# Cross-attention and expert layer: setup and attention loop laid out anew over five batches a step

## The reference, cut to what matters

```python
x = x + attention(layernorm(x), ctx, mask, Wq, Wk, Wv, Wo)   # x: 16 x 256 x 128, ctx: 16 x 64 x 128
x = x + experts(layernorm(x), gate_w, wi_gate, wi_up, wo)

def attention(H, T, mask, Wq, Wk, Wv, Wo):                   # 16 heads of 8
    q, k, v = shape(H @ Wq) * 8 ** -0.5, shape(T @ Wk), shape(T @ Wv)
    scores = q @ k.T + (1 - mask) * finfo.min
    return (softmax(scores) @ v) @ Wo

def experts(x, ...):                                         # 8 experts, F = 512, top 2
    probs, idx = top_k(softmax(x @ gate_w.T), 2); probs /= sum(probs)
    for k in range(2):                                       # capacity 640 tokens for each k and expert
        pos = running count of the tokens that chose the same expert
        out += where(pos < 640, probs[k] * (silu(x @ wi_gate) * (x @ wi_up)) @ wo of expert idx[k], 0)
```

## Time and profile before

| | |
|---|---|
| median of 3 runs | 415.29 us (413.87 to 417.47) |
| profiled execution, its own time | 416.42 us |
| its span, first to last instruction | 414.6 us |
| mean granted TensorE clock | 0.946 |
| busy: TensorE, DVE, GpSimd, ACT | 359.5, 259.9, 228.2, 189.4 us |

### The profile page before, as it was taken

The page is one execution under the profiler, slowest core; times in us unless marked ns, Lnnn a source line. Parts: engine busy times, 40 slices in busy tenths (PEclk is TensorE's granted clock), DMA queues, the critical chain, the costliest instruction groups (busy, mean ns, idle before and its releaser), DMA issues.

```text
span 414.6 us, 8885 instructions
## 1 busy us (share of the span) xinstructions
PE 359.5 (87%) x3012; PEld 311.1 (75%) x3012; DVE 259.9 (63%) x893; ACT 189.4 (46%) x430; POOL 228.2 (55%) x190
## 2 busy tenths in 40 slices
PE   0776889999989999648499999999999999999980
PEld 0465567667766676337399999999999999999980
DVE  4947868988898989754144545565554546555430
ACT  2435647667757677422132443443443434344320
POOL 9514421035337757877207648386565837747664
PEclk9969959999999999967799999999999999999996
DMA  8898010122212322111503444636345463544332
GB/s 257 249 326 280 6 31 14 20 48 73 39 43 67 83 74 72 60 58 54 148 4 26 91 97 38 162 33 146 48 53 140 37 161 26 121 73 37 29 28 25
DMA packets 41958, 35.05 MB, mean 85 GB/s; under 512 B 9136, under 2 KB 38320, under 8 KB 41776
## 3 DMA queue, kind: packets, MB, share of 16 engines
q1 hardware_dynamic: 27824, 24.72, 21.2%
q0 software_dynamic: 13568, 9.58, 16.9%
q10 hardware_dynamic: 528, 0.27, 0.2%
HBM read 21.64 MB, written 17.73 MB: 95 GB/s over the span
## 4 chain that ended last, share of the span: by engine, by line
PE 64%; DVE 17%; POOL 7%; issue 5%; DMA 2%; ACT 2%; POOLq 0%; DVEq 0%; ACTq 0%
PE bank L820 17%; PE bank L629 10%; PE bank L631 9%; PE bank L630 9%; POOL slots L443 6%; PE bank L706 4%; DVE mneg L925 3%; PE bank L658 2%; PE bank L672 2%; DVE rall L1044 2%; PE bank L685 2%; PE bank L811 2%; PE bank L793 1%; PE bank L686 1%; PE bank L696 1%
## 5 line engine op out<-in xcount | busy, mean ns | idle before, releaser
L477 POOL DMA_INDIRECT out<-ys,idx x80 | 124.9, 1561 | 84.4 <-DVE ys L1123 36.8
L1150 DVE TENSOR_TENSOR h<-sg,bank 128x256 f32<-128x256 f32 x160 | 66.0, 417 | 87.5 <-ACT sg L614 79.2
L614 ACT ACTIVATE sg<-bank 128x256 f32<-128x256 f32 x160 | 61.6, 385 | 108.1 <-PE bank L631 107.2
L629 PE MATMUL bank<-ex_hi,w_hi 128*128 128x256 f32 x320 | 96.1, 300 | 1.1 <-DVE ex_lo L1104 0.3
L630 PE MATMUL bank<-ex_hi,w_lo 128*128 128x256 f32 x320 | 89.7, 280 | 0.0
L631 PE MATMUL bank<-ex_lo,w_hi 128*128 128x256 f32 x320 | 89.7, 280 | 0.0
L820 PE MATMUL bank<-w_raw,h 128*128 128x128 f32 x640 | 78.0, 275 | 0.8 <-DVE h L1150 0.8
L820 PEld LDWEIGHTS bank<-w_raw,h 128*128 128x128 f32 x640 | 74.9, 192 | 0.9 <-DVE h L1150 0.9
L443 POOL DMA_INDIRECT slots<-rall,slot x64 | 64.0, 1000 | 19.6 <-issue 15.2
L629 PEld LDWEIGHTS bank<-ex_hi,w_hi 128*128 128x128 f32 x320 | 61.1, 191 | 4.2 <-issue 2.5
L630 PEld LDWEIGHTS bank<-ex_hi,w_lo 128*128 128x128 f32 x320 | 61.2, 191 | 0.0
(11 more groups left out here) (120 smaller groups left out, 540.5 us busy)
## 6 DMA issues: line engine op xcount, KB each, us to landing
slots<-in_empty SPq DMA_DIRECT2D x8, 660.0 KB, 10.1
xl<-slots SPq DMA_DIRECT2D x7, 660.0 KB, 6.8
w_raw<-in_wgu SPq DMA_DIRECT2D x8, 512.0 KB, 3.8
X<-in_x SPq DMA_DIRECT2D x4, 512.0 KB, 7.7
w_raw<-in_wdn SPq DMA_DIRECT2D x8, 256.0 KB, 4.3
out<-X SPq DMA_DIRECT2D x16, 128.0 KB
out<-ys,idx POOLq DMA_INDIRECT x80, 3.3
ks<-kc SPq DMA_DIRECT2D x72, 16.0 KB
```

What stands on the lines that cost most here:

```text
L477: nc.gpsimd.indirect_dma_start(out=out[:, :], out_offset=bass.IndirectOffsetOnAxis(ap=IDX[v][:, j:j + 1], axis=0), in_=YS[c][:, t, :], in_ ...
L614: nc.scalar.activation(SG[m % 2][:], GATE_PS[m % 2][:, 0:2 * P], ACT.Silu).then_inc(sg_ready, 1)
L629: nc.tensor.matmul(ps, hi, m_hi, start=True, stop=False)
L1150: nc.vector.tensor_tensor(H[n % 2][:, f, :], SG[m % 2][:], UP_PS[m % 2][:, 0:2 * P], ALU.mult).then_inc(h_ready, 1)
```

## The change

The loop runs over steps 0 to 19, and each step works on five batches: i + 1 and i as before; batch i - 1 for all four blocks of `scores` and `exps`, its sums and its weighted values; batch i - 2 for output, second normalisation and its sum with the input; batch i - 3 for its turned rows and gate logits. In each engine the order of the step is new. `row_scores(i + 1, 0)` stands at the end of step i.

Setup: the broadcast mask is replaced by two small loads (one transposed, counted by a product with ones); ctx and X come in pieces, wk, const and wq from ACT's queue; keys are projected for batches 0 to 7 ahead of the loop and for 8 to 15 in steps 0 and 1, two groups a step; values in four groups, two of them in step 0. The moments of the first normalisation are taken four tiles at a time, in the steps that MOMENTS names. Queries are projected by one fp32 product (its operand a plain copy, so the subtraction at L1023 goes). Eleven products on ones stand ahead of the key projection (WARM0). There are 6 key buffers. GpSimd's first six `spread_keys` fill them, SP places from batch 6 on.

Routing: BLOCKS is four blocks of two batches and eight of one; a block's choice is made in its ROUTED step, its rank at that step's end and its slots in the step after, with tiles doubled so that two blocks can be under way. SENDS now counts single sends; the waits by which `milestone` (L426) spaced them are gone.

```diff
-KBUF = 4
+KBUF = 6
 VROW = 2 * 144
-BLOCKS = [(0, 3), (3, 4), (7, 3), (10, 2), (12, 1), (13, 1), (14, 1), (15, 1)]
+BLOCKS = [(0, 2), (2, 2), (4, 2), (6, 2)] + [(b, 1) for b in range(8, 16)]
 ROUTED = {first + n + 2: m for m, (first, n) in enumerate(BLOCKS)}
-POINTS = [(0,), (1,), (2,), (3,), (4,), (5,), (), (), (), (6, 7), (8, 9), (10, 11, 12, 13, 14, 15)]
-DRAIN = [(), (0, 1, 2, 3, 4, 5), (), (), (6, 7, 8, 9, 10, 11, 12, 13, 14, 15), (), (), (), (), (), (), ()]
-SENDS = {6: 2, 7: 2, 8: 1, 9: 1, 10: 3, 11: 3, 12: 2, 13: 3, 14: 3, 15: 3, 16: 3, 17: 2, 18: 2, 19: 2}
+RT = 4
+SENDS = {5: 4, 6: 3, 7: 5, 8: 3, 9: 5, 10: 4, 11: 5, 12: 5, 13: 5, 14: 5, 15: 4, 16: 4, 18: 12}
+MOMENTS = {0: 2, 1: 3, 2: 4, 3: 5, 5: 6, 7: 7}
+WARM0 = (4, 7)
...
-        K_PS = [MX[0], MX[1], QP, DEN_PS]
+        K_PS = [MX[0], MX[1], DEN_PS, M1, M1, M1, M1, M1]
...
+            sp.dma_start(MASKT[:], maskt).then_inc(maskt_in, 16)
+            sp.dma_start(CTX[:, 0:8, :], ctx[:, 0:8, :]).then_inc(ctx_in[0], 16)
+            sp.dma_start(X[:, 0:4, :], x_t[:, 0:4, :]).then_inc(x_in[0], 16)
+            sp.dma_start(MASKR[:], mask).then_inc(maskr_in, 16)
+            sp.dma_start(CTX[:, 8:16, :], ctx[:, 8:16, :]).then_inc(ctx_in[1], 16)
             sp.dma_start(WV[:], wv).then_inc(w_in, 16)
+            sp.dma_start(X[:, 4:8, :], x_t[:, 4:8, :]).then_inc(x_in[1], 16)
             for q in range(1, 4):
-                sp.dma_start(X[:, 8 * q:8 * q + 8, :], x_t[:, 8 * q:8 * q + 8, :]).then_inc(x_in[q], 16)
+                sp.dma_start(X[:, 8 * q:8 * q + 8, :], x_t[:, 8 * q:8 * q + 8, :]).then_inc(x_in[q + 1], 16)
             sp.dma_start(WO[:], wo).then_inc(w_in, 16)
             sp.dma_start(GATE[:], gate).then_inc(w_in, 16)
-            sp.wait_ge(setup, 5)
-            sp.wait_ge(pool_setup, 1)
+            sp.wait_ge(ext_step, 2)
+            sp.wait_ge(kc_set, 2)
             for g in range(GROUPS):
-                sp.dma_start(KC[ONE_ROW:ONE_ROW + 1, :, g, :], MASKF[ONE_ROW:ONE_ROW + 1]).then_inc(ext_in, 16)
+                sp.dma_start(KC[ONE_ROW:ONE_ROW + 1, :, g, :], EXT[:]).then_inc(ext_in, 16)
...
+            clear_values(1)
+            pool.wait_ge(pool_setup, 1)
+            inverse_deviation(0)
+            pool.wait_ge(const_in, 16)
+            pool.wait_ge(k_used, 4)
+            pool.wait_ge(ext_in, 64)
+            spread_keys(0)
+            inverse_deviation(1)
+            clear_values(2)
+            clear_values(3)
+            spread_keys(1)
...
+            def step(i):
+                if i + 2 < KBUF:
+                    spread_keys(i + 2)
+                if there(i - 2):
+                    inverse_deviation2(i - 2)
+                if i in MOMENTS:
+                    inverse_deviation(MOMENTS[i])
...
+                first = sum(n for at, n in SENDS.items() if at < i)
+                for n in range(first, first + SENDS.get(i, 0)):
+                    send(n)
...
+            act.dma_start(WK[:], wk).then_inc(wk_in, 16)
+            act.dma_start(C[:], const).then_inc(const_in, 16)
+            act.dma_start(WQ[:], wq).then_inc(wq_in, 16)
...
+            context_hi(0)
+            act.wait_ge(const_in, 16)
+            act.wait_ge(sel_clear, 1)
+            ident_g = IDENT.rearrange("p (g c) -> p g c", g=GROUPS)
+            for part, sel in ((0, SEL_HI), (2, SEL_HI), (1, SEL_LO)):
+                ins = nc.scalar.copy(sel[:, :, part, :], ident_g)
+            ins.then_inc(sel_ready, 1)
+            for n in range(4):
+                keys_hi(n)
+            keep_turned(0)
+            keep_values(0)
+            queries_hi(0)
+            stack_queries(0, 0)
+            stack_queries(0, 1)
+            keep_values(1)
+            context_hi(1)
+            def step(i):
+                if there(i + 1):
+                    keep_turned(i + 1)
+                if there(i - 3):
+                    keep_turned2(i - 3)
+                if there(i - 1):
+                    exps(i - 1, 0)
+                if i in (0, 1):
+                    keys_hi(2 * i + 4)
+                if there(i + 1):
+                    queries_hi(i + 1)
+                if i == 0:
                     keep_values(2)
+                if there(i - 1):
+                    exps(i - 1, 1)
+                    exps(i - 1, 2)
+                    exps(i - 1, 3)
+                if i - 1 in ROUTED:
+                    weights_of(ROUTED[i - 1])
+                if i == 0:
                     keep_values(3)
+                if there(i + 1):
+                    stack_queries(i + 1, 0)
+                if there(i - 1):
+                    log_sums(i - 1)
+                    guesses(i - 1)
+                if i in (0, 1):
+                    keys_hi(2 * i + 5)
+                if there(i):
+                    keep_maxima(i)
+                if there(i + 1):
+                    stack_queries(i + 1, 1)
...
+            def queries(b):
+                pe.wait_ge(xt_ready, b + 1)
+                nc.tensor.matmul(M0[:, 0:LQ], WQ[:], XT[b % 2][:], start=True, stop=True).then_inc(q_full, 1)
...
+            pe.wait_ge(ones_set, 1)
+            keep_warm(WARM0[0])
+            pe.wait_ge(maskb_ready, 1)
+            nc.tensor.matmul(ST[0][:, 0:B], ONES[0:LK, :], MASKB[:], start=True, stop=True).then_inc(count_full, 1)
+            keep_warm(WARM0[1])
+            for n in range(4):
+                project_keys(n)
+            pe.wait_ge(const_in, 16)
+            turn(0)
+            pe.wait_ge(any_ready, 1)
+            project_values(0)
+            pe.wait_ge(wq_in, 16)
+            queries(0)
+            project_values(1)
+            pe.wait_ge(sel_ready, 1)
+            select(0, 0)
+            select(0, 1)
+            pe.wait_ge(v2_first, 2)
+            pe.wait_ge(kc_set, 3)
+            row_scores(0, 0)
+            def step(i):
+                if there(i + 1):
+                    turn(i + 1)
+                if there(i - 3):
+                    turn2(i - 3)
+                if there(i - 1):
+                    scores(i - 1, 0)
+                if there(i):
+                    row_scores(i, 1)
+                if i in (0, 1):
+                    project_keys(2 * i + 4)
+                if there(i + 1):
+                    queries(i + 1)
+                if there(i - 1):
+                    scores(i - 1, 1)
+                if there(i - 3):
+                    gate_logits(i - 3)
+                if there(i):
+                    row_scores(i, 2)
+                if i == 0:
                     project_values(2)
+                if there(i - 1):
+                    scores(i - 1, 2)
+                if there(i):
+                    row_scores(i, 3)
+                if i == 0:
                     project_values(3)
+                if there(i - 1):
+                    scores(i - 1, 3)
+                if there(i - 2):
+                    output(i - 2)
+                if there(i + 1):
+                    select(i + 1, 0)
+                if there(i - 1):
+                    sums(i - 1)
+                if i in (0, 1):
+                    project_keys(2 * i + 5)
+                if there(i):
+                    turn_maxima(i)
+                if there(i + 1):
+                    select(i + 1, 1)
+                    row_scores(i + 1, 0)
+                if there(i - 1):
+                    values(i - 1, 0).then_inc(pv_full, 1)
+                if i in ROUTED:
+                    rank(ROUTED[i], i)
+            over_steps(step)
...
+            mask_context(0)
+            dve.wait_ge(wk_hi_ready, 1)
+            nc.vector.tensor_tensor(WK_LO[:], WK[:], WK_HI[:].bitcast(F32), ALU.subtract).then_inc(wk_lo_ready, 1)
+            dve.wait_ge(anyr_ready, 1)
+            dve.wait_ge(ext_step, 1)
+            nc.vector.tensor_scalar(EXT[:], EXT[:], ANYR[:, 0:1], None, ALU.mult).then_inc(ext_step, 1)
+            context_lo(0)
+            moments(0)
+            keys_lo(0)
+            norm(0)
+            norm(1)
+            for n in range(1, 4):
+                keys_lo(n)
+            queries_lo(0)
+            moments(1)
+            mask_context(1)
+            row_max(0, 0)
+            context_lo(1)
+            def step(i):
+                now, last = ROUTED.get(i), ROUTED.get(i - 1)
+                if there(i):
+                    row_max(i, 1)
+                if last is not None:
+                    if last == 0:
+                        dve.wait_ge(tables, 3)
+                    own_ranks(last)
+                if i == 0:
+                    norm(2)
+                if there(i + 1):
+                    queries_lo(i + 1)
+                if there(i - 3):
+                    keep_logits(i - 3)
+                if there(i):
+                    row_max(i, 2)
+                if i in (0, 1):
+                    keys_lo(2 * i + 4)
+                if there(i):
+                    row_max(i, 3)
+                if there(i - 2):
+                    add_input(i - 2)
+                if last is not None:
```

(47 more changed lines are left out.)

914 lines of the change are left out of this document (399 added, 515 removed).

## The result

The changed kernel takes 427.81 us (median of 4 runs, 425.72 to 429.2); the kernel before, timed beside it, 416.25. The ratio is 1.0297, with a 95% interval of 1.026 to 1.0334: slower. The forecast was 409.7 us, with a range of 397 to 421. A ratio compares the fast executions of both kernels, while a median is of all executions, so that the two can differ where some were slow. The profiled execution of the changed kernel took 425.72 us, its span is 423.9 and its mean granted clock 0.934.

What follows compares the result with a forecast made beforehand. Steps were taken as bound by TensorE's ordered work plus its wait for ScalarE's chain, 9.0 us each. Lead -10.5, steps +4.9, tail unchanged: -5.6, so 410.8 us profiled and 409.7 median, range 397 to 421.

Steps and rivals of the forecast that it cites:

- The setup: Before the loop: first row scores at 20.5 us, 12.7 earlier; batch 0's maxima turned at 27.0, a lead of 10.5.
- The four key groups: In the setup: key projections from about 8 us, ending at about 13.5, with two normalisations between them.
- The chain of the new step: ScalarE's logarithm, guess, maxima copy, stacking: row scores 3.54 us after the sums; TensorE waits 1.7 us each step.
- A plain step: In the loop, a step without added moments: 4.0 + 3.54 + 1.44 = 9.0 us.
- The moments: VectorE, 1.3 us for four tiles ahead of the second row maximum: fourth row scores 0.6 later in three steps.
- The sum: Whole kernel: -10.5 at batch 0, +4.9 over fifteen steps, tail unchanged; together -5.6, so 410.8 us for the profiled execution.
- GpSimd's 7.2 us of work: In the loop: at most 5 x 1.26 + 0.92 = 7.2 us a step, under 9.0, so not the bound.
- The clock: In the steps: TensorE's work taken at full-clock durations, with nothing in the forecast for falls.
- The clock falls in the steps: Rival, 0.17: the 1.7 us waits make TensorE's clock fall, about 4 us each; three falls give 422 us.
- The tail: After the last turned maxima, until the last send ends: 30.2 us against 30.9 before, called no change.
- The steps are not longer: Rival, 0.28: free changes of form and half the stacking wait make steps 8.4 us; with a warm setup, 400 us.
- VectorE and GpSimd block each other: Rival, 0.10: more normalisations meet key spreads before the middle of step 3; four more of 1.6 us give 416.

Runs made afterwards that it cites:

- the run with idle products: The changed kernel with four idle TensorE products in the wait before the next row scores, no clock falls in its steps: 417.19 us, ratio 1.004.

## Why the prediction was wrong

**The setup** was right: first row scores 20.25 (20.5), maxima of batch 0 at 27.4 (27.0). It was partly right by luck. The replicated mask landed late, and the first key product started at 9.55, not 8, as the chain of waits shows (start, duration):

```profile
2.47 4.38 DMA maskr<-in_mask
...
9.55 0.74 PE bank L671
...
14.08 0.22 PE bank L709 x2
14.30 0.14 issue
14.44 1.11 PE bank L700 x16
```

The four key groups then took 4.5 us and not 5.5, since nothing came between them: their products stand 0.43 us or more apart up to 12.86, and 0.23 from 13.16 on. So the value products began at 14.44 after all, and a group cost 1.1, not the cold 1.8. From the first row scores to the maxima of batch 0 it is then 7.1 us (6.5), and 10.0 in the run with idle products, where the clock fell in that stretch.

**The chain of the new step** was right: row scores start 9.16 - 5.5 = 3.66 us behind the sums (3.54), and the wait is 1.7 to 1.8 us (1.7). A plain step is 9.16 to 9.3 us (9.0), so it was undersized by 0.26. Over the thirteen steps between the first and the last that is 3.4 us.

**The moments** were undersized. The sum had 0.6 in three steps and 0.5 in one, 2.3 in all. The run without falls shows 9.68 to 9.89 in five steps where 9.26 is plain, which is 2.9 us, 0.6 more. Of the rest of the 5.7 us, 1.1 is the ninth step, 0.3 the last and 0.2 the seventh. The ninth is an overlap that the prediction had wrong: it compared GpSimd's 7.2 us of work with a step of 9.0 and found room, but not the order of that work, in which moments that come late hold up five sends and the power behind them.

**The clock** is the step that failed. The sum entered the new wait as 1.7 us of time and all of TensorE's work at its full-clock durations, so that it had nothing for falls in the fifteen steps; the runs show nine falls there, worth 10.8 us. "The clock falls in the steps" stood as a rival with 0.17, and it is what happened. The prediction had the evidence, a wait of 1.63 us with 0.70 around it, and a new wait of 1.7 us in every step. It counted the fuller work on both sides as a reason against, and priced a fall at 4 us from a single one that had lasted 10 us. The sizes were off in opposite ways: nine falls, not three, at 1.2 us, not 4. That their product, 10.8 us, is near that rival's 12 is luck. A wait that comes back in every step should have had more of the chance.

**The tail** was called no change against 30.9 us. The last send ends 28.9 us behind the last maxima, where the working had 30.2. Three powers and twenty sends were left, as forecast; but the first power starts 0.4 us behind the maxima and not 1.2, and no send is slowed by the 1.04 that was added for one. Two of its rows (GpSimd, timeline):

```profile
181.74 1.03 POOL L440 DMA_INDIRECT slots<-rall,slot  x1 [0.20 <-issue]
...
208.38 0.96 POOL L440 DMA_INDIRECT slots<-rall,slot  x1 [0.30 <-issue]
```

Together: +0.4 at batch 0, +16.5 in the steps (10.8 clock, 5.7 the rest), -2.0 in the tail, so 14.9 us, by which the profiled execution missed its forecast of 410.8. The median missed 409.7 by 18.1.

**The other rivals.** "The steps are not longer" fell: each link of the chain kept its length. That VectorE and GpSimd block each other showed in step 0 at 22.6, where a pair of normalisations took 1.68 us beside a key spread; the next two pairs took 0.60 each, and the sum above leaves nothing for it to explain.

## What to carry to other kernels

A wait that the new order puts into every step costs its own length and, on TensorE, it can cost what the clock loses behind it: look at whether it comes back each step, not at how busy the step is on average. First ask which work queued behind the waiting instruction doesn't need what is waited for. On an engine that also serves a second chain, look at the order of its work and not only at its sum. Here one move of 1.0 us of products ahead of the wait was worth 5.6% (ratio 1.0297 to 0.9718), and with the maxima and the moments moved too the kernel is 5.3% faster than before. A gain won in the setup is only kept if the steps behind it stay as short as they were, so time the steps by themselves.

## What the runs showed of the hardware

- A wait of 1.8 us in a step of 9 us was enough for the granted clock to fall from 1.00 to 0.50 in seven to nine of fifteen steps, in three executions that no stall disturbed. It did not come each time: in another execution four steps with the whole wait, from 47 to 86 us, kept 1.00. Four products of 0.26 us in the middle of the wait (0.92 us of waiting left) kept it at 1.00 for all fifteen.
- At half clock TensorE's sixteen small products took 1.94 us instead of 1.07, and a stretch of 3.4 us cost a step 1.4 to 1.5 us where TensorE alone set its length, and 0.4 to 0.9 where TensorE would have waited for VectorE otherwise.
- Chips differ. The kernel before took 415 us on one and 430 to 432 on three others. On one of those the changed kernel, with its 64 indirect sends of about 1.26 us beside the steps, took 176.1 us for the steps, and 151.6 with the sends behind them; on the quiet chip, with them behind, the steps took 150.1 us, and beside the falls only one step was seen to differ, by 1.1 us. A comparison with several variants therefore needs its own kernel before on the same chip, and a look at the single steps.
